# Two expert layers computed for sorted token-expert pairs in blocks of 128, in place of eight dense experts

## Chip, cores and metric

The kernel runs on one core of one Trainium2 chip. Its time is the device time of one execution, in microseconds (us). A core has TensorE (PE, matmuls; the load of their stationary operand is PEld), VectorE (DVE), ScalarE (ACT), GpSimd (POOL) and SyncE (SP, which here only issues transfers), each with a queue of its own that it works off strictly in order. They meet by semaphores.

## The reference, cut to what matters

The input is x, 4 sequences of 512 tokens of 128 numbers, in float32. Eight layers follow one another, each as x = x + layer(layernorm(x)): 0 a state space with 16 heads, 1 a feed forward, 2 a Mamba block, 3 experts with gelu, 4 linear attention with 16 heads, 5 a ternary feed forward, 6 a scan (called the last scan here), 7 experts with a silu gate. The two expert layers are what changes:

```
# layer 3: 8 experts, 128 -> 512 -> 128, the two most probable of each token count
probs = softmax(x @ Wr.T); topv, topi = top_k(probs, 2)
combine = sum(topv[..., None] * one_hot(topi, 8), axis=2)
for each expert e:  h = gelu(x @ w1[e] + b1[e]);  y = h @ w2[e] + b2[e]
                    out += combine[..., e, None] * y
# layer 7: the same with topv / sum(topv), and
g = x @ w_gate[e] + b_gate[e];  u = x @ w_up[e] + b_up[e]
y = (silu(g) * u) @ w_down[e] + b_down[e];  out += combine[..., e, None] * y
```

Written like this every expert is computed for every token, though only two of eight weights in `combine` differ from zero.

## The kernel before

**Tiles and streams.** P = 128, T = 512 tokens of a sequence, NC = 4 chunks of 128 tokens. x stays in SBUF (`x0` to `x3`). Two sequences are worked on at once, as stream 0 and stream 1; sequences 0 and 1 go through all eight layers (the first round), then 2 and 3 (the second round, with the same buffers). Each stream has four PSUM banks. In the tables of the trace buffer numbers are left out: `big`, `cv`, `mt`, `up`, `key`, `xT` stand for tiles that both streams have.

**What sets the order.** For every engine a layer is a generator that yields before each step. `walk(engine, programs)` runs the generators of both streams through each other by a table `RUNS[engine]`: the lengths of alternating runs of steps, stream 0, stream 1, stream 0 and so on. So each engine's queue is a fixed interleaving of two streams, written down ahead. Nothing overtakes at run time: a step that waits holds all that stands behind it on its engine, of the other stream too. The same helper `expert_loads()` gives the order in which SP brings expert weights into `expert_ring`, four slots for both streams.

**An expert layer before.** The layer norm and its transposes give `xT` (features on partitions, 512 tokens). `route` makes the logits (PE L1557), the softmax and the two largest (DVE L1172 to L1192), and spreads them as weights of eight experts, `cmb` (DVE L1196 and L1199). PE transposes `cmb` (L1562), ACT copies it (L748), and PE multiplies it with the experts' second biases (L1363, out of `rows8`). Then for each of the 8 experts:

- gelu layer: four matmuls 128x512 (L1606), four ACT activations 128x512 (L760), `down`: 16 matmuls 128x128 (L1363, by `by_token`), and on DVE `gated_sum`, four operations 128x128 that add the result times the token's weight to x (L1214).
- silu layer: eight matmuls 128x512 (L1626), four activations (L773), four DVE products 128x512 (L1237), then `down` and `gated_sum` as above.

A matmul in float32 is two instructions in the trace. SP loads 512 KB (gelu) or 768 KB (silu) for each expert.

**The other layers** that the text speaks of: a Mamba block is 16 steps a stream of DVE scans (L1137), a product (L1147) and POOL work (L563, L551), and ends in the output matmul (PE L1363 out of `weights` and `big`); attention works in eight groups of two heads (one PE L1643 each, among others), the ternary layer is mostly PE L1685, the state space has PE L1415, the last scan L1697 and others. POOL L517 computes the layer norms' 1/sqrt.

Of the kernel before, what the change touches and what calls it, by code (L numbers as in the profile page):

```python
# [35 lines left out]
NE = 8  # L36
DI = 1024
# [18 lines left out]
for _k, _w in WCOLS:  # L56
# [6 lines left out]
         ("mb1", 32), ("w1_s", 4), ("w2_s", 4), ("h1_s", 4), ("h2_s", 4), ("normw", 2),  # L63
         ("bg", 32), ("bu", 32), ("alpha", 1), ("beta", 1), ("a0", 1), ("w3_s", P)]
# [7 lines left out]
CCOLS = [("ident", P), ("tri", T), ("iota8", NE), ("pos", T), ("m_ref", REF + 64), ("mod128", T),  # L72
# [4 lines left out]
for _k, _w in CCOLS:  # L77
# [14 lines left out]
RING = 4  # L92

# [68 lines left out]
def expert_loads():  # L162

    met = [0] * NS
    order = []
    for s in turns("loads"):
        n = met[s] // NE
        order.append((n % 2, s + NS * (n // 2), met[s] % NE))
        met[s] += 1
    return order  # L170
# [1673 lines left out]
```

## Time and profile before

| | us |
|---|---|
| median of 3 runs | 1624.49 (1623.52 to 1625.1) |
| the profiled execution | 1621.69 |
| its span in the trace | 1619.8 |
| granted TensorE clock, mean | 0.911 of full speed |

The profile's first part gives each engine's busy time and instructions. Its second part cuts the span into 40 slices of 40.5 us, with a digit for the busy tenths of each engine, and PEclk for the clock that TensorE was granted. The chain that ended last is followed back from the last instruction; "issue" in it is time in which the engine waited for nothing that the profile shows. In the groups of instructions each row has the operation, its tiles and shapes, the count, then busy time, the mean of one in ns, and the idle time of the engine just before them with what ended most of it.

### The profile page before, as it was taken

What the parts mean: (1) busy time and instruction counts of PE and PEld (TensorE: products, weight loads), DVE (VectorE), ACT (ScalarE), POOL (GpSimd) and SP (SyncE); (2) the same over time, 40 slices, a digit from 0 to 9 for tenths busy, and PEclk for the clock granted to TensorE, in tenths of its full rate; (3) what the DMA queues carried; (4) which work ended last, traced back from release to release, by engine and by line L of the source; (5) the groups of instructions that cost most, each with busy time, mean ns of one, the idle gap of its engine ahead of it and who ended that gap; (6) DMA issues with size and microseconds to landing.
All of it is one profiled execution on the core that took longest, in us unless ns stands there. A gap on an engine that the chain in (4) does not pass through costs nothing.

```text
span 1619.8 us, 15913 instructions
## 1 busy us (share of the span) xinstructions
PE 1364.0 (84%) x5628; PEld 812.9 (50%) x5628; DVE 992.1 (61%) x2001; ACT 742.7 (46%) x1083; POOL 227.6 (14%) x192
## 2 busy tenths in 40 slices
PE   1986754569999979999689987998797799998998
PEld 0534511136766555655364554566333475555665
DVE  4676699978562464425647996457998427513533
ACT  1532474348434333244546873753586533234322
POOL 0100025634000000010001441000144000000000
PEclk9997866669999998999899997999898899997999
DMA  7000000001112000210001110110000021100211
GB/s 311 0 1 0 1 0 0 1 0 53 53 39 72 20 0 20 79 59 0 1 1 39 40 39 14 39 42 25 1 1 0 14 79 39 39 20 20 79 59 46
DMA packets 13446, 54.51 MB, mean 34 GB/s; under 512 B 1320, under 2 KB 3496, under 8 KB 12976
## 3 DMA queue, kind: packets, MB, share of 16 engines
q1 hardware_dynamic: 12784, 48.55, 9.1%
q10 hardware_dynamic: 576, 4.87, 0.7%
q8 instruction: 47, 0.77, 0.2%
q14 instruction: 39, 0.32, 0.1%
HBM read 52.37 MB, written 1.05 MB: 33 GB/s over the span
## 4 chain that ended last, share of the span: by engine, by line
PE 57%; DVE 11%; ACT 8%; issue 4%; POOL 1%; DVEq 0%; ACTq 0%; POOLq 0%
PE ps L1363 16%; PE ps L1626 12%; PE ps L1606 6%; PE ps L1685 5%; DVE up L1137 2%; PE ps L1415 2%; PE ps L1655 2%; PE ps L1674 2%; PE ps L1723 1%; PE ps L1643 1%; PE ps L1527 1%; PE ps L1354 1%; PE ps L1697 1%; ACT L739 1%; DVE big L1147 1%
## 5 line engine op out<-in xcount | busy, mean ns | idle before, releaser
L1363 PEld LDWEIGHTS ps<-expert_ring,big 128*128 128x128 f32 x2048 | 239.6, 193 | 32.4 <-issue 25.4
L1626 PE MATMUL ps<-xT,expert_ring 128*128 128x512 f32 x512 | 241.4, 611 | 12.6 <-ACT cv L773 9.9
L1363 PE MATMUL ps<-expert_ring,big 128*128 128x128 f32 x2048 | 241.0, 276 | 5.0 <-DVE x L1214 5.0
L517 POOL TENSOR_TENSOR rstd<-ve,nhalf 128x4 f32<-128x4 f32 x44 | 47.7, 1085 | 1010.7 <-DVE ve L931 843.6
L1137 DVE TENSOR_TENSOR_SCAN up<-cv,big 128x512 f32<-128x512 f32 x128 | 173.1, 1392 | 9.1 <-ACT cv L739 8.1
L1214 DVE SCALAR_TENSOR_TENSOR x<-ps,cmb,x 128x128 f32<-128x128 f32 x256 | 71.8, 342 | 171.0 <-PE ps L1363 170.2
L773 ACT ACTIVATE cv<-ps,params 128x512 f32<-128x512 f32 x128 | 86.8, 687 | 177.4 <-PE ps L1626 177.2
L1626 PEld LDWEIGHTS ps<-xT,expert_ring 128*128 128x128 f32 x512 | 94.4, 193 | 123.6 <-issue 95.1
L1237 DVE SCALAR_TENSOR_TENSOR big<-ps,params,cv 128x512 f32<-128x512 f32 x128 | 95.0, 746 | 84.6 <-PE ps L1626 82.1
L760 ACT ACTIVATE big<-ps,params 128x512 f32<-128x512 f32 x128 | 85.8, 687 | 95.6 <-PE ps L1606 95.0
L1606 PE MATMUL ps<-xT,expert_ring 128*128 128x512 f32 x256 | 126.6, 619 | 3.1 <-ACT big L760 2.8
L1544 PE MATMUL ps<-q,row_pick 96*128 96x512 bf16 x128 | 57.0, 459 | 72.8 <-DVE big L1147 51.8
L563 POOL TENSOR_TENSOR big<-big,mt 128x512 f32<-128x512 f32 x64 | 86.4, 1351 | 220.1 <-DVE up L1137 134.3
L1685 PE MATMUL ps<-big,weights 128*128 128x512 f32 x256 | 115.6, 593 | 0.0
L739 ACT ACTIVATE cv<-big,nega 128x512 f32<-128x512 f32 x128 | 88.2, 716 | 19.6 <-DVE up L1137 17.5
L1363 PE MATMUL ps<-weights,big 128*128 128x128 f32 x608 | 80.3, 290 | 12.9 <-DVE big L1160 8.7
L1363 PEld LDWEIGHTS ps<-weights,big 128*128 128x128 f32 x608 | 76.6, 204 | 25.7 <-DVE big L1160 10.3
L1527 PE MATMUL ps<-big,consts 128*128 128x512 f32 x128 | 83.3, 738 | 4.3 <-DVE big L1147 4.3
L551 POOL TENSOR_TENSOR mt<-mt,big 128x512 f32<-128x512 f32 x60 | 78.5, 1310 | 35.2 <-DVE big L1147 34.9
L1655 PE MATMUL ps<-qkv_parts,selectors_rounded 128*128 128x512 f32 x192 | 72.7, 490 | 9.6 <-DVE up L1273 7.0
L1544 PEld LDWEIGHTS ps<-q,row_pick 96*128 96x128 bf16 x128 | 13.8, 109 | 133.0 <-DVE big L1147 82.2
L1415 PE MATMUL ps<-big,mt 128*128 128x512 f32 x160 | 74.0, 619 | 2.7 <-ACT big L641 2.7
(232 smaller groups left out, 2010.6 us busy)
## 6 DMA issues: line engine op xcount, KB each, us to landing
expert_ring<-in_e_dram SPq DMA_DIRECT2D x32, 768.0 KB, 4.3
expert_ring<-in_e_dram SPq DMA_DIRECT2D x32, 512.0 KB, 3.6
weights<-in_w_dram ACTq DMA_DIRECT2D x1, 3072.0 KB, 13.3
weights<-in_w_dram SPq DMA_DIRECT2D x1, 1600.0 KB, 13.6
big<-in_sel_dram SPq DMA_DIRECT2D x1, 1024.0 KB, 7.6
x<-in_x_dram SPq DMA_DIRECT2D x4, 256.0 KB, 12.2
out_dram<-x SPq DMA_DIRECT2D x4, 256.0 KB, 5.7
big<-in_c_dram SPq DMA_DIRECT2D x1, 1008.0 KB, 10.2
```

The source lines that it names most:

```text
L563: pool.tensor_tensor(BIG2[s][:, 1, :], BIG1[s][:, 3, :], MT[s][:, 0:T], ALU.mult).then_inc(m_d1[s], 1)
L739: act.activation(CV[s][:, j, :], BIG1[s][:, j, :], ACT.Exp, scale=nega[:, j * NM + n:j * NM + n + 1]).then_inc(m_da[s], 1)
L773: act.activation(CV[s][:, k % 2, :], bank(s, (8 * e + 2 * k) % 3), ACT.Silu, bias=pr("bg", 4 * e + k)).then_inc(g.act[s], 1)
L1137: dve.tensor_tensor_scan(UP[s][:, j, PAD:PAD + T], CV[s][:, j, :], BIG2[s][:, j, :], 0.0, ALU.mult, ALU.add).then_inc(m_scan[s], 1)
L1237: dve.scalar_tensor_tensor(BIG1[s][:, 4 * (e % 2) + k, :], bank(s, (8 * e + 2 * k + 1) % 3), pr("bu", 4 * e + k), CV[s][:, k % 2, :], ALU. ...
L1363: last = pe.matmul(bank4(s, k)[:, c, :], lhs(b, c), rhs(b), start=(b == 0), stop=(b == blocks - 1))
L1415: last = pe.matmul(bank(s, c), MT[s][:, m:m + P], BIG2[s][:, k, :], start=(k == 0), stop=(k == c))
L1527: pe.matmul(bank(s, 0), ident, BIG2[s][:, 2, :], start=(n == 0), stop=(n == NM - 1))\
L1606: pe.matmul(bank(s, k % 3), ring[:, slot, k * P:(k + 1) * P], XT[s][:, PAD:PAD + T], start=True, stop=True).then_inc(g.up[s], 1)
L1626: pe.matmul(bank(s, b % 3), ring[:, slot, r * T + k * P:r * T + (k + 1) * P], XT[s][:, PAD:PAD + T], start=True, stop=True).then_inc(g.up[ ...
L1655: last = pe.matmul(bank(s, k), SELR[:, m * P:(m + 1) * P], PARTS[:, part, src, :], start=(part == 0), stop=(part == 1))
L1685: last = pe.matmul(bank(s, j), w(name, (4 * b + j) * P, P), BIG1[s][:, src + b, :], start=(b == 0), stop=(b == 3))
```

## The change

Both expert layers compute only the chosen token-expert pairs, 1024 for a sequence. NBLK = 15 blocks of 128 slots each hold pairs of one expert: 1024/128 = 8 full blocks and up to 7 more since each expert's last block may be partly filled. Which expert a block belongs to is known only at run time.

- `route` ends otherwise: DVE makes one-hots of the two choices (`oneh`, `chosen`); PE counts and ranks them with small bfloat16 matmuls (a triangle `trib`, ones `oneb`); some 13 small DVE operations turn that into the expert of each block (`whoi`) and each pair's slot (`posu`, 8 columns of 128). The transposes of `cmb`, its copy and the bias matmul go.
- POOL issues 8 indirect transfers (L653) that scatter the normalised tokens (`cv`) to rows of a DRAM buffer `slots0` or `slots1`, one a stream; SP reads them back in 4 transfers (L567), PE transposes 15 blocks (L1720), ACT copies them (L847).
- For each block SP loads the expert's number from SBUF into a register (L559), and issues the weights' transfer at that address (L561): 592 KB for gelu, 856 KB for silu, both biases included. PE: 4 (gelu) or 8 (silu) matmuls 128x128 (L1761), ACT 4 activations 128x128 (L876, L873), for silu 4 DVE products 128x128 (L1373), PE 4 matmuls 128x128 (L1734), DVE one addition of the bias into `YS` (L1337). 
- SP writes the results to a DRAM buffer in 4 transfers (L571), POOL gathers each token's two results with 8 indirect transfers (L660) into `up`, and DVE adds them to x by 8 operations 128x128 (L1346).
- SP clears both slot buffers once at the start, 983 KB each. The ring's slot frees when `result` has been computed (`y`) instead of with the down matmuls (`dn`).
- All tables in RUNS are new, for the other layers too; "loads" becomes "sp", an order of all that SP does.

```diff
+NBLK = 2 * T // P + NE - 1
+SP_MOE = ["w0", "w1", "x0", "x1", "x2", "x3", "w2", "w3", "w4", "w5", "w6", "w7", "y0", "w8", "w9", "w10", "w11",
+          "y1", "w12", "w13", "w14", "y2", "y3"]
 RUNS = {
...
-    "loads": [
-        8, 8, 8, 8, 8, 8, 8, 8],
+    "sp": [
+        1, 1, 21, 1, 1, 1, 1, 21, 19, 2, 4, 8, 1, 14, 23, 23, 19, 2, 4, 8, 1, 14],
 }
...
 SP:
-                    sp.wait_ge(moe[pm].dn[pi], moe[pm].dn.at(pi, pe_))
-                dst = ring[:, q % RING, :] if m else ring[:, q % RING, 0:1024]
-                sp.dma_start(dst, (e3_d if m else e1_d)[e]).then_inc(ring_in[q % RING], 16)
+                            if n == 0:
+                                sp.wait_ge(g.eb[s], g.eb.at(s, 0))
+                            if q >= RING:
+                                pm, pi, pb = loads[q - RING]
+                                sp.wait_ge(moe[pm].y[pi], moe[pm].y.at(pi, pb))
+                            e = sp.value_load(whoi[s][0:1, n:n + 1], min_val=0, max_val=NE - 1)
+                            src = (e3_d if m else e1_d)[bass.ds(e, 1)].rearrange("o p n -> p (o n)")
+                            sp.dma_start(ring[:, q % RING, 0:EW[m]], src).then_inc(ring_in[q % RING], 16)
...
+                        if label[0] == "x":
+                            if n == 0:
+                                sp.wait_ge(scattered[s % NS], 128 * (nth_moe(m, s) + 1))
...
 POOL:
+                    for j in range(2 * NC):
...
+                        pool.indirect_dma_start(xs_d[k], bass.IndirectOffsetOnAxis(ap=posu[s][:, j:j + 1], axis=0),
+                                                XH[s][:, j % NC, :], None).then_inc(scattered[k], 16)
+                    for j in range(2 * NC):
...
+                        pool.indirect_dma_start(YG[s][:, j // NC, (j % NC) * P:(j % NC + 1) * P], None, ys_d[k],
+                                                bass.IndirectOffsetOnAxis(ap=posu[s][:, j:j + 1], axis=0))\
...
 DVE:
-                for e in range(NE):
-                    if e:
-                        yield from gated_sum(0, s, e - 1)
-                yield from gated_sum(0, s, NE - 1)
+                for b in range(NBLK):
+                    yield from result(0, s, b)
+                yield from gated_sum(0, s)
...
 PE:
+                            if r == 0:
+                                pe.wait_ge(ring_in[q % RING], 16 * (q // RING + 1))
+                                if b % 4 == 0:
+                                    pe.wait_ge(g.gt[s], g.gt.at(s, b // 4))
+                                if m and b:
+                                    pe.wait_ge(g.act[s], g.act.at(s, b - 1))
+                            elif b:
+                                pe.wait_ge(g.h[s], g.h.at(s, b - 1))
+                            for k in range(4):
+                                last = pe.matmul(bank4(s, r if m else b % 2)[:, k, :],
+                                                 ring[:, q % RING, r * T + k * P:r * T + (k + 1) * P],
+                                                 XGT[s][:, b // 4, b % 4 * P:(b % 4 + 1) * P], start=True, stop=True)
```

What stands in a row on PE, first round, from the Mamba output of stream 0 (`weights,big2_0`) into its gelu experts, beside stream 1's Mamba steps (`row_pick`, `big2_1`). Before:

```order
L1363 MATMUL ps<-weights,big2_0 128x128 x8
L1544 MATMUL ps<-q128_1,row_pick 128x512
L1527 MATMUL ps<-big2_1,consts 128x512
L1544 MATMUL ps<-q128_1,row_pick 128x512
L1354 MATMUL ps<-consts,cv0 128x128 x4
L1557 MATMUL ps<-weights,xT0 128x8 x4
L1544 MATMUL ps<-q128_1,row_pick 128x512
L1527 MATMUL ps<-big2_1,consts 128x512
L1544 MATMUL ps<-q128_1,row_pick 128x512
L1562 MATMUL ps<-consts,cmb0 8x128 x4
L1363 MATMUL ps<-rows8,bT0 128x128 x4
L1606 MATMUL ps<-xT0,expert_ring 128x512 x2
```

After, where the slots of stream 0 are transposed and its first blocks start:

```order
L1681 MATMUL ps<-q128_1,row_pick 128x512 x2
L1664 MATMUL ps<-big2_1,consts 128x512
L1681 MATMUL ps<-q128_1,row_pick 128x512 x2
L1664 MATMUL ps<-big2_1,consts 128x512
L1720 MATMUL ps<-consts,big2_0 128x128 x8
L1761 MATMUL ps<-big1_0,expert_ring 128x128 x4
L1720 MATMUL ps<-consts,big2_0 128x128 x7
L1761 MATMUL ps<-big1_0,expert_ring 128x128 x4
L1664 MATMUL ps<-big2_1,consts 128x512
L1734 MATMUL ps<-expert_ring,big1_0 128x128 x4
L1761 MATMUL ps<-big1_0,expert_ring 128x128 x4
L1734 MATMUL ps<-expert_ring,big1_0 128x128 x4
```

The experts of stream 0 now begin late in stream 1's Mamba steps, behind a transfer to DRAM and back, and stand among its last steps.

What stands in a row on PE near the end of the program, the silu experts of stream 0 and then of stream 1. Before:

```order
L1363 MATMUL ps<-rows8,bT1 128x128 x4
L1626 MATMUL ps<-xT1,expert_ring 128x512
L1363 MATMUL ps<-expert_ring,big1_0 128x128 x16
L1626 MATMUL ps<-xT1,expert_ring 128x512 x15
L1363 MATMUL ps<-expert_ring,big1_1 128x128 x16
L1626 MATMUL ps<-xT1,expert_ring 128x512 x8
L1363 MATMUL ps<-expert_ring,big1_1 128x128 x16
```

After:

```order
L1761 MATMUL ps<-big1_0,expert_ring 128x128 x8
L1734 MATMUL ps<-expert_ring,big1_0 128x128 x8
L1720 MATMUL ps<-consts,big2_1 128x128 x8
L1761 MATMUL ps<-big1_1,expert_ring 128x128 x8
L1720 MATMUL ps<-consts,big2_1 128x128 x7
L1761 MATMUL ps<-big1_1,expert_ring 128x128 x8
L1734 MATMUL ps<-expert_ring,big1_1 128x128 x4
```

Before, stream 1's experts follow on stream 0's; after, all 15 blocks of stream 1 stand alone behind the last of stream 0, and the first waits for the slots to come back.

What stands in a row on POOL at the end of the program. Before:

```order
L517 TENSOR_TENSOR rstd0<-ve0,nhalf 128x4
L551 TENSOR_TENSOR mt1<-mt1,big2_1 128x512
L517 TENSOR_TENSOR rstd1<-ve1,nhalf 128x4
L517 TENSOR_TENSOR rstd0<-ve0,nhalf 128x4 x2
L517 TENSOR_TENSOR rstd1<-ve1,nhalf 128x4 x5
```

After:

```order
L589 TENSOR_TENSOR rstd0<-ve0,nhalf 128x4 x3
L589 TENSOR_TENSOR rstd1<-ve1,nhalf 128x4
L653 DMA slots0_dram<-cv0,key0 1920x128 x8
L589 TENSOR_TENSOR rstd1<-ve1,nhalf 128x4 x3
L653 DMA slots1_dram<-cv1,key1 1920x128 x8
L660 DMA up0<-results0_dram,key0 128x128 x8
L660 DMA up1<-results1_dram,key1 128x128 x8
```

Where only the layer norms' operations stood, 32 indirect transfers stand between and behind them, and a gather of one stream can stand behind a scatter of the other.

## Rows read from the trace of the kernel before

**Rows 1.** The page's first part, engines, and its second part's granted clock.

```profile
PE 1364.0 (84%) x5628; PEld 812.9 (50%) x5628; DVE 992.1 (61%) x2001; ACT 742.7 (46%) x1083; POOL 227.6 (14%) x192
...
PEclk9997866669999998999899997999898899997999
```

**Rows 2.** The page's costliest groups of instructions; columns as told above.

```profile
L1626 PE MATMUL ps<-xT,expert_ring 128*128 128x512 f32 x512 | 241.4, 611 | 12.6 <-ACT cv L773 9.9
L1363 PE MATMUL ps<-expert_ring,big 128*128 128x128 f32 x2048 | 241.0, 276 | 5.0 <-DVE x L1214 5.0
...
L1214 DVE SCALAR_TENSOR_TENSOR x<-ps,cmb,x 128x128 f32<-128x128 f32 x256 | 71.8, 342 | 171.0 <-PE ps L1363 170.2
...
L1237 DVE SCALAR_TENSOR_TENSOR big<-ps,params,cv 128x512 f32<-128x512 f32 x128 | 95.0, 746 | 84.6 <-PE ps L1626 82.1
...
L1606 PE MATMUL ps<-xT,expert_ring 128*128 128x512 f32 x256 | 126.6, 619 | 3.1 <-ACT big L760 2.8
```

**Rows 3.** The chain of waits: start, length, what; two stretches late in the program.

```profile
1411.08 27.47 PE ps L1685 x64
...
1600.41 6.87 PE ps L1626 x16
1607.29 3.58 PE ps L1363 x32
```

**Rows 4.** The page's DMA issues: count, KB each, us from issue to landing.

```profile
expert_ring<-in_e_dram SPq DMA_DIRECT2D x32, 768.0 KB, 4.3
expert_ring<-in_e_dram SPq DMA_DIRECT2D x32, 512.0 KB, 3.6
```

**Rows 5.** Timeline, Mamba output to the first expert: start, length, engine, operation.

```profile
328.41 3.78 PE L1363 MATMUL ps<-weights,big 128*128 128x128 f32 x16 [5.50 <-DVE big L1160]
...
339.45 1.87 PE L1557 MATMUL ps<-weights,xT 128*128 128x8 f32 x8 [0.69 <-ACT xT L625]
...
342.50 0.18 DVE L1178 RECIPROCAL sm<-sm 128x4 f32<-128x4 f32 x1
342.71 0.19 DVE L1179 TENSOR_TENSOR lg<-lg,sm 128x32 f32<-128x32 f32 x1
...
344.02 0.18 DVE L1192 CAST topf<-topi 128x32 f32<-128x32 uint32 x1
...
349.86 1.22 PE L1606 MATMUL ps<-xT,expert_ring 128*128 128x512 f32 x1
```

**Rows 6.** Timeline of POOL, one operation in two places.

```profile
211.07 1.27 POOL L563 TENSOR_TENSOR big<-big,mt 128x512 f32<-128x512 f32 x1 [4.70 <-DVE big L1124]
...
278.17 2.03 POOL L563 TENSOR_TENSOR big<-big,mt 128x512 f32<-128x512 f32 x1 [1.22 <-DVE up L1137]
```

**Rows 7.** All transfers that store the output: us to landing.

```profile
DMA to landing us min/median/max: 2.3/5.7/5.8
```

**Rows 8.** Timeline of PE: attention groups, the last scan, the state space's start and second product.

```profile
561.72 1.02 PE L1643 MATMUL ps<-up,selectors 128*128 128x512 f32 x2
562.58 3.60 PE L1697 MATMUL ps<-xT,weights 128*128 128x512 f32 x8
...
571.80 1.02 PE L1643 MATMUL ps<-up,selectors 128*128 128x512 f32 x2
...
598.56 2.03 PE L1363 MATMUL ps<-weights,big 128*128 128x128 f32 x16
...
710.92 0.60 PE L1354 MATMUL ps<-consts,cv 128*128 128x128 f32 x4
...
787.22 10.46 PE L1415 MATMUL ps<-big,mt 128*128 128x512 f32 x20 [0.69 <-ACT big L641]
```

**Rows 9.** Windows: length, busy (count) of PE, PEld, DVE, ACT, POOL, clock, DMA share, GB/s.

```profile
40.00:200.00 160.00, 129.45 (x518) 76.50 (x517) 103.82 (x204) 63.65 (x101) 14.79 (x16) 0.88 0.00 1
208.00:408.00 200.00, 127.60 (x393) 61.88 (x394) 183.12 (x233) 108.85 (x156) 88.93 (x64) 0.72 0.04 11
```

**Rows 10.** Timeline of DVE at the start, behind a register load and a branch.

```profile
32.67 0.87 DVE L936 BATCH_NORM_STATS2 stat<-x 128x6 f32<-128x128 f32 x4 [7.24 <-issue]
```

More of the change, by code:

```diff
@@ L162, in expert_loads, with network @@
 def expert_loads():
+    labels = [[None] + [(m, i, label) for i in range(k, NB, NS) for m in range(2)
+                        for label in SP_MOE + ["out"] * m] for k in range(NS)]
     met = [0] * NS
     order = []
[L166 to L169, printed above, removed]
+    for k in turns("sp"):
+        if met[k] < len(labels[k]):
+            label = labels[k][met[k]]
+            if label and label[2][0] == "w":
+                order.append((label[0], label[1], int(label[2][1:])))
+        met[k] += 1
     return order
-def network(nc, x_d, w_d, p_d, c_d, sel_d, a_d, e1_d, e3_d, r8_d, out_d, layers=NLAYERS):
+def network(nc, x_d, w_d, p_d, c_d, sel_d, a_d, e1_d, e3_d, r8_d, xs_d, ys_d, out_d, layers=NLAYERS):
     ctx = ExitStack()
@@ new lines, in route @@
+                step(dve.tensor_reduce(used, cnt4[s][:, :, :], AX.X, ALU.add))
+                step(dve.tensor_tensor_scan(ends, ones[:, 0:1].broadcast_to([P, NE]), used, 0.0, ALU.mult, ALU.add))
+                dve.tensor_tensor(past[s][:, :, :], ends[0:1].unsqueeze(1).broadcast_to([1, NBLK, NE]),
+                                  cn("blocks", 1)[:, 0:NBLK].unsqueeze(2).broadcast_to([1, NBLK, NE]), ALU.is_le)
+                step(dve.tensor_tensor(first, ends, used, ALU.subtract))
+                dve.tensor_reduce(whof[s][:, 0:NBLK], past[s][:, :, :], AX.X, ALU.add)
@@ new lines, in result, with gated_sum @@
+                dve.tensor_tensor(YS[s][:, group % 2, cols], bank4(s, 2 + b % 2)[:, 0, :], ring[:, slot, EW[m] - P:EW[m]],
+                                  ALU.add)\
+                    .then_inc(g.y[s], 1)
+            def gated_sum(m, s):
+                for r in range(2):
+                    yield
+                    dve.wait_ge(gathered[s % NS][r], 64 * (nth_moe(m, s) + 1))
+                    for c in range(NC):
+                        last = dve.scalar_tensor_tensor(X[s][:, c, :], YG[s][:, r, c * P:(c + 1) * P],
+                                                        top[s][:, c, r:r + 1], X[s][:, c, :], ALU.mult, ALU.add)
+                    if r == 0:
+                        step(last)
+                    else:
+                        last.then_inc(x_done[7 if m else 3][s], 1)
@@ L1612, in experts_silu @@
[L1612 to L1630 removed]
+                pe.wait_ge(g.mk[s], g.mk.at(s, 0))
@@ new lines, in route, with turn_slots @@
+                last.then_inc(g.rk[s], 1)
+            loads = expert_loads()
+            def turn_slots(g, s, k):
+                yield
+                pe.wait_ge(xg_in[s % NS][k], 16 * (nth_moe(moe.index(g), s) + 1))
+                if k >= 2:
+                    pe.wait_ge(g.gt[s], g.gt.at(s, k - 2))
+                elif k == 1:
+                    pe.wait_ge(g.pos[s], g.pos.at(s, 0))
+                for b in range(min(4, NBLK - 4 * k)):
+                    last = pe.transpose(bank4(s, 2 + k % 2)[:, b, :], XG[s][:, k, b * P:(b + 1) * P], ident)
+                last.then_inc(g.tr[s], 1)
@@ new lines, in down @@
+            def down(m, s, b):
+                g = moe[m]
+                wd = ring[:, loads.index((m, s, b)) % RING, 512 * (m + 1):512 * (m + 2)]
+                yield
+                hidden = g.h if m else g.act
+                pe.wait_ge(hidden[s], hidden.at(s, b))
+                if b >= 2:
+                    pe.wait_ge(g.y[s], g.y.at(s, b - 2))
+                else:
+                    pe.wait_ge(g.gt[s], g.gt.at(s, 2 + b))
+                for k in range(4):
+                    last = pe.matmul(bank4(s, 2 + b % 2)[:, 0, :], HID[s][:, b % 4, k * P:(k + 1) * P],
+                                     wd[:, k * P:(k + 1) * P], start=(k == 0), stop=(k == 3))
+                last.then_inc(g.dn[s], 1)
@@ L1750, in _ @@
                 first_block_general(pe, "pe", state_space(True))
-            walk("pe", [state_space(False), feed_forward, mamba, experts_gelu, attention, ternary, last_scan,
-                         experts_silu])
+            walk("pe", [state_space(False), feed_forward, mamba, experts(0, "r1"), attention, ternary, last_scan,
+                         experts(1, "r3")])
 def layout(i):
```

370 lines of the change are left out of this document (215 added, 155 removed), and 72 rows, old and new, of the table RUNS.

## The prediction, written before the changed kernel ran

> **What bounds the kernel now.** Read first the busy shares [rows 1]: TensorE 1364.0 of the span's 1619.8 us, no other engine near. Then the granted clock [rows 1]: where its digit is 6, PE is the less busy engine and DVE the busy one (in the window 208:408 DVE 183.12 of 200, PE 127.60, clock 0.72) [rows 9]; so the Mamba stretches are DVE's, nearly all the rest PE's. Then the costliest groups [rows 2]: the expert layers are 241.4 + 126.6 + 241.0 = 609 us of PE. The chain near its end [rows 3] shows them back to back: 6.87 up and 3.58 down for each silu expert, no gap. There a matmul less is time less.
>
> **What goes.** An old silu expert is 10.44 us of PE, a gelu expert 3.44 + 3.57 = 7.0 (half the up matmuls of rows 3). DVE loses 71.8 + 95.0 [rows 2].
>
> **What comes, on PE.** 16 matmuls 128x128 take 3.58 (x32 there, two records each) [rows 3], 0.223 each. A new gelu block has 8, 1.79 us; a silu block 12, 2.68; 30 + 30 blocks and 120 transposes of 0.15 or so: some 300 us with the group's mean of 0.235 for the 1200 (241.0/1024). PE busy falls from 1364 to about 1065. If PE alone set the time, the gain would be 300 us; I expect less than half of it, because each expert layer now holds a round trip that no engine computes in.
>
> **Routing.** From the start of the Mamba output to `topf` 15.6 us (328.41 to 344.02) and to the first expert 21.4 [rows 5]. New behind `topf`: about 14 dependent small DVE operations at 0.21 from one to the next (342.50 to 342.71), a small PE step with two hops, ~5 in all. Positions stand at +20.6; bounds 18 to 24, with up to three of the other stream's DVE operations of about a microsecond between them.
>
> **The round trip.** No row shows an indirect transfer. The nearest rows of POOL's queue are its own operations: L563, 1.27 alone and 2.03 beside a busy DVE [rows 6]. A zero-cost issue would be the lower end, and nothing excludes it; I take 1.3, the undisturbed row of the same engine for a 128-row operation, with bounds 0.4 to 2.03. Eight are 10.4, and landing 2.3 (the shortest of the stores) [rows 7]: 12.7 for a scatter and for a gather. Slots come back in 3, transposes and copy 1.7. Positions to first block 17.4, so Mamba output to first block 38 (21.4 before). Behind the last block: last down and its addition 1.2, result write 2.7 (0.4 more than the 2.3), gather 12.7, eight additions at 0.342 (L1214) [rows 2] 2.7: **19 us**, against four such, 1.4, before. POOL's queue behind a scatter holds the other stream's 1/sqrt of the layer norm (the order on POOL), up to 10 us; most of those are far apart.
>
> **SP.** Each block adds a register load and an issue, in one queue for both streams. The nearest row is DVE's 7.24 at the start, a register load with a branch [rows 10]; the lower end is an ordinary issue, ~0.35. I take 1.0. The Trainium skill, "DMA: Bandwidth & Descriptors" (Latency and other measured facts), gives a `tensor_load` a floor of about 600 ns; no run here shows it, and by it the loads would hide. Weights: 592 and 856 KB against 512 in 3.6 and 768 in 4.3 [rows 4], where 256 KB more cost 0.7: so 3.8 and 4.5 to land, and 1.6 and 2.3 of the transfer engines each, below a block's pace. 87 MB in all (41 before) is no limit.
>
> **Pace of blocks.** In-order downs and the ring of four tie block q to block q-4: SP 1.35, landing 3.8 or 4.5, up 0.9 or 1.8, four activations of 128 columns 1.4 (taken as DVE's of that width), down 0.9, addition 0.3: 8.7, and for silu 11.6 with DVE's four products. Over four blocks that is 2.2 and 2.9; with hops **2.4 for gelu, 3.0 for silu**; bounds 1.8 and 2.7 (PE) to 3 and 3.6. Eight old experts were 56 and 84; fifteen blocks are 36 and 45. Alone, a gelu layer goes 21.4 + 56 + 1.4 = 79 to 38 + 36 + 19 = 93, longer; a silu layer 107 to 102. What is won is PE time for the other stream during the round trips, so the gain hangs on what stands beside them. Therefore a walk through the new orders.
>
> **The walk.** Legs from rows: two of attention's eight groups in 10.1 (561.72 to 571.80) [rows 8], eight 40, some 10 around them, 7 for the layer norm (332.2, the output matmul's end, to 339.45) [rows 5]: 57; ternary 32 matmuls 27.47 [rows 3], 40 with the tail and layer norm 45 to 53; last scan 36 (562.58 to 598.56) [rows 8], 42 to 51 with what surrounds it; state space to its second product 76 (710.92 to 787.22) [rows 8], 32 more to its output; DVE per stream for state space and feed forward 103.82/2 = 52, for a Mamba block ~88 [rows 9].
> First round: the Mamba output of stream 0 comes at 345 (328 before: the new order on PE lets stream 1 go ahead by some 3.5 steps, at 88/16 less its share of other work about 4.7 each). Slots 388 (38, and 5 behind stream 1's steps in the order on PE); blocks to 424; x 443; attention 500; ternary 553; last scan 598; ternary of stream 1 to 638; its scan 689; its slots 727. Stream 0's silu blocks run meanwhile and give x at 735; its second-round state space starts at 742, second product 818. Stream 1's last downs stand behind that product: 829; state space out 850.
> Second round: Mamba of stream 0 beside state space and feed forward of stream 1, DVE 88 + 52, with its waits 145: 995. Slots 1033, blocks 1069, x 1088, attention 1145. Stream 1's Mamba output 1135, slots 1173, blocks 1209, rest of ternary 0 to 1233, last scan 1282, ternary 1 to 1330, its scan 1381, slots 1419, fifteen silu blocks alone to 1464, gather and sum 1483, store 2.4 [rows 7] 1485; and the 1.9 by which the profiled time (1621.69) exceeds its span: **1487**, against 1621.69, whose distance to the median of 1624.49 is 0.2%.
> As a cross-check: 1065 of PE in 1487 is 72%, so the gaps grow from 256 to 422 us. The granted clock would then fall: windows with PE near 64% show 0.72 [rows 9]. A fall of mean clock from 0.91 to 0.87 costs 5% of about 600 us where PE binds, 30 us, inside my range.
>
> **The rivals.** (a) POOL is held by DVE. If the indirect transfers behave as L563 beside DVE, 2.03 each [rows 6], the walk holds nine groups of eight: 72 x 0.75 = 54, **1541**. For it: round trips stand beside Mamba steps, where DVE is at 92%. Against: the last ones stand where DVE idles. The Trainium skill, "DMA: Bandwidth & Descriptors" (SWDGE vs HWDGE vs iDMA), says GpSimd writes such descriptors into SBUF and that DVE locks it out in its two-port modes; no row of before has such a transfer to show it.
> (b) Blocks at PE's pace and cheap transfers: 0.6 less for each of the 30 gelu blocks on the path of the second round and 0.3 for some 30 silu blocks, 27, and 0.7 for each of 72 transfers, 50: **1410**. For it: nothing in the trace forbids an issue of 0.6.
> (c) Slower: the register load on SP, price p for each block. SP then gives one slot every p + 0.35, for both streams; a block lasts 2.4 to 3.0, so up to p = 2.2 nothing changes, and above it about 90 block times on the path grow. The gain of 138 is used up at 138/90 = 1.5 more, p about 4. At the 7.2 of rows 10 the 60 blocks of the two lone stretches and the shared ones cost 90 x 4.7 = 420: **1905**. Against it: those 7.24 have a branch and a start in them, and no row shows a load by itself that dear.
> (d) The exchange doesn't pay: orders that hold a stream's work behind the other's slots eat the gain, round trips growing by 17 us in all eight layers (8 x 17 = 136): **1622**, no change.
>
> **How the numbers follow.** Forecast 0.60 (its own range 1445 to 1530), (a) 0.14, (b) 0.13, (c) 0.08, (d) 0.05. The range 1395 to 1580 takes in the forecast, (a), (b) and their bounds and leaves out (c), (d) and the tails: about 8 in 10. Faster by over 0.2% (about what a measurement of this kernel can tell from no change): 0.60 + 0.14 + 0.13 + half of (d) = 0.89; within 0.2%: 0.01; slower: 0.10.
>
> **What would show it.** PE busy 1040 to 1090, DVE about as before (it loses 167, gains some 130 in blocks and sums). POOL's timeline: eight transfers in 9 to 12 us (a: above 16). Between the last `topf` and the first L1761: 20 to 25. Block pace in the last silu layer: 3.0; if it is 4 or more and the ring's landing ends the waits, (c). The last 19 us of the span: no PE. In the second round the Mamba stretch of DVE should stand nearly as before; if it shrinks or grows by over 20 us, my legs are wrong, not the prices. Wrong I would also be if a scatter to DRAM took far longer to land than the 2.3 of a plain store: 5 us more would be 9 x 5 = 45.

## The result, and the profile after

| | before | after |
|---|---|---|
| median, us | 1625.10 (1622.38 to 1629.41, 15 runs) | 1634.78 (1627.51 to 1639.36, 15 runs) |
| ratio | | 1.0046, 95% interval 1.003 to 1.0062 |
| span of the profiled execution | 1619.8 | 1633.4 |
| granted TensorE clock, mean | 0.911 | 0.826 |

The changed kernel is half a per cent slower, by more than its interval. The forecast was 1487. All times here and below are of undisturbed executions, two to eight for most versions; of `ring8_small` there is only one (its other ran at a granted clock of 0.594 and took 2057).

The page's first part and the granted clock, after (they answer to [rows 1]):

```profile
PE 1157.1 (71%) x5300; PEld 760.8 (47%) x5300; DVE 955.1 (58%) x2083; ACT 646.5 (40%) x1274; POOL 369.1 (23%) x321
...
PEclk9998757556998989886897777767877998897788
```

TensorE lost 207 us of busy time, and more than that came back as idle time: 476 us without a matmul against 256. The clock is below full through most of the program. Its costliest groups and the issues of weights (to [rows 2] and [rows 4]):

```profile
L1761 PE MATMUL ps<-big,expert_ring 128*128 128x128 f32 x1440 | 212.0, 300 | 97.8 <-DMA expert_ring<-in_e_dram 80.7
...
L1734 PE MATMUL ps<-expert_ring,big 128*128 128x128 f32 x960 | 130.5, 280 | 8.5 <-ACT big L876 7.4
...
L660 POOL DMA_INDIRECT up<-results_dram,key x64 | 62.4, 975 | 219.2 <-DMA results_dram<-mt 199.5
...
L653 POOL DMA_INDIRECT slots_dram<-cv,key x64 | 66.1, 1033 | 103.3 <-DVE key L1324 86.8
...
expert_ring<-in_e_dram SPq DMA_DIRECT2D x60, 836.0 KB, 4.7
expert_ring<-in_e_dram SPq DMA_DIRECT2D x60, 578.0 KB, 4.6
```

The first row's last part is the news: 97.8 us in which PE stood idle ahead of a block's up matmuls, 80.7 of them for expert weights to land. Before, experts' matmuls waited 12.6 + 3.1 + 5.0 us in all [rows 2], and PE's list of waits has none for a load of weights.

Where the time went along the program, read from the start of each layer norm's transposes on PE (L1354 before, L1491 after; an apostrophe marks the second round; the forecast's column is its walk, with the 7 to 10 us of a layer norm added where it named the end of a layer). The last two columns are versions told of below:

| start of | before | forecast | after | sp_order | ring5 |
|---|---|---|---|---|---|
| attention, stream 0 | 437 | 450 | 464 | 465 | 458 |
| state space', stream 0 | 711 | 742 | 794 | 765 | 749 |
| feed forward', stream 0 | 842 | 857 | 898 | 870 | 851 |
| gelu experts', stream 0 | 991 | 1005 | 1086 | 1056 | 1037 |
| attention', stream 0 | 1105 | 1095 | 1194 | 1163 | 1145 |
| silu experts', stream 1 | 1505 | 1388 | 1506 | 1472 | 1449 |
| end | 1620 | 1485 | 1633 | 1570 | 1541 |

The forecast's lead is lost in three places: 38 us ahead of the second round (stream 0's and stream 1's silu experts), 40 between feed forward' and gelu experts', 30 behind the last layer norm; the rest in pieces of 14 to 19, less 11 that the state space' wins back.

### The profile page after: what moved, and what is told of

Read it like the earlier page. It is cut to its first block and busy times, and to the rows that moved or that the text cites. A ratio compares the mean times of both kernels' runs of the same rounds, so it can differ in the third digit from the quotient of the medians.

```text
span 1633.4 us, 16356 instructions
## 1 busy us (share of the span) xinstructions
PE 1157.1 (71%) x5300; PEld 760.8 (47%) x5300; DVE 955.1 (58%) x2083; ACT 646.5 (40%) x1274; POOL 369.1 (23%) x321
## 5 line engine op out<-in xcount | busy, mean ns | idle before, releaser
L1761 PE MATMUL ps<-big,expert_ring 128*128 128x128 f32 x1440 | 212.0, 300 | 97.8 <-DMA expert_ring<-in_e_dram 80.7
L1761 PEld LDWEIGHTS ps<-big,expert_ring 128*128 128x128 f32 x1440 | 193.3, 211 | 115.4 <-DMA expert_ring<-in_e_dram 89.8
L1244 DVE TENSOR_TENSOR_SCAN up<-cv,big 128x512 f32<-128x512 f32 x128 | 181.4, 1456 | 15.3 <-POOL big L635 12.2
L1373 DVE SCALAR_TENSOR_TENSOR big<-ps,expert_ring,key 128x128 f32<-128x128 f32 x240 | 67.6, 344 | 140.4 <-PE ps L1761 125.3
L635 POOL TENSOR_TENSOR big<-big,mt 128x512 f32<-128x512 f32 x64 | 87.9, 1379 | 226.2 <-ACT mt L828 114.7
L1734 PE MATMUL ps<-expert_ring,big 128*128 128x128 f32 x960 | 130.5, 280 | 8.5 <-ACT big L876 7.4
L1734 PEld LDWEIGHTS ps<-expert_ring,big 128*128 128x128 f32 x960 | 120.5, 196 | 17.3 <-ACT big L876 12.8
L873 ACT ACTIVATE key<-ps,expert_ring 128x128 f32<-128x128 f32 x240 | 68.4, 368 | 147.5 <-PE ps L1761 147.1
L660 POOL DMA_INDIRECT up<-results_dram,key x64 | 62.4, 975 | 219.2 <-DMA results_dram<-mt 199.5
L828 ACT ACTIVATE mt<-ps 128x512 f32<-128x512 f32 x64 | 38.4, 600 | 144.9 <-PE ps L1681 123.2
L1337 DVE TENSOR_TENSOR mt<-ps,expert_ring 128x128 f32<-128x128 f32 x120 | 34.3, 287 | 98.1 <-PE ps L1734 97.8
L653 POOL DMA_INDIRECT slots_dram<-cv,key x64 | 66.1, 1033 | 103.3 <-DVE key L1324 86.8
L876 ACT ACTIVATE big<-ps,expert_ring 128x128 f32<-128x128 f32 x240 | 67.9, 374 | 53.2 <-PE ps L1761 53.0
```

The source lines that it names most:

```text
L635: pool.tensor_tensor(BIG2[s][:, 1, :], BIG1[s][:, 3, :], MT[s][:, 0:T], ALU.mult).then_inc(m_d1[s], 1)
L873: last = act.activation(SG[s][:, b % 2, cols], bank(s, 0)[:, cols], ACT.Silu, bias=bias[:, k:k + 1])
L876: last = act.activation(HID[s][:, b % 4, cols], bank(s, b % 2)[:, cols], ACT.Gelu, bias=bias[:, k:k + 1])
L1244: dve.tensor_tensor_scan(UP[s][:, j, PAD:PAD + T], CV[s][:, j, :], BIG2[s][:, j, :], 0.0, ALU.mult, ALU.add).then_inc(m_scan[s], 1)
L1734: last = pe.matmul(bank4(s, 2 + b % 2)[:, 0, :], HID[s][:, b % 4, k * P:(k + 1) * P], wd[:, k * P:(k + 1) * P], start=(k == 0), stop=(k == 3))
L1761: last = pe.matmul(bank4(s, r if m else b % 2)[:, k, :], ring[:, q % RING, r * T + k * P:r * T + (k + 1) * P], XGT[s][:, b // 4, b % 4 * P ...
```

## Experiments

Times are medians; "after" is 1634.8. A difference of a few us between two versions with two executions each is within the spread. Kernels that leave work out say so in their expectation.

### Whose slots: the order on SP

The end of the program in after. First SP's issues of weights from 1506 on (start, length, queue, operation), then DVE's results of blocks 11 and 12 of stream 0, each of which frees a slot, and PE's up matmuls with their waits:

```profile
1508.58 0.33 SPq L561 DMA_DIRECT2D expert_ring<-in_e_dram  x1
...
1516.95 0.33 SPq L561 DMA_DIRECT2D expert_ring<-in_e_dram  x1
...
1518.12 2.74 SPq L561 DMA_DIRECT2D expert_ring<-in_e_dram  x2
...
1534.37 0.34 SPq L561 DMA_DIRECT2D expert_ring<-in_e_dram  x1
```

```profile
1519.48 0.28 DVE L1337 TENSOR_TENSOR mt<-ps,expert_ring 128x128 f32<-128x128 f32 x1
...
1528.17 3.79 PE L1761 MATMUL ps<-big,expert_ring 128*128 128x128 f32 x16 [8.88 <-DMA expert_ring<-in_e_dram]
...
1533.03 0.28 DVE L1337 TENSOR_TENSOR mt<-ps,expert_ring 128x128 f32<-128x128 f32 x1
...
1539.38 3.41 PE L1761 MATMUL ps<-big,expert_ring 128*128 128x128 f32 x16 [6.44 <-DMA expert_ring<-in_e_dram]
...
1562.93 3.58 PE L1761 MATMUL ps<-big,expert_ring 128*128 128x128 f32 x16 [5.79 <-DMA expert_ring<-in_e_dram]
...
1573.25 3.54 PE L1761 MATMUL ps<-big,expert_ring 128*128 128x128 f32 x16 [5.85 <-DMA expert_ring<-in_e_dram]
```

Read them together. At 1508.58 SP loads block 12 of stream 0; at 1516.95 and 1518.12 come blocks 0 and 1 of **stream 1**, whose slots in DRAM are not even written yet. PE starts on the first of them at 1550.67, 34 us later, and their slots are loaded anew only at 1558.51 and 1568.66: two of the four slots are held all that time. So stream 0's block 13 may load only when block 11 is done (1519.48; PE runs block 13 at 1528), and block 14 when block 12 is done (1533.03; PE runs block 14 at 1539). PE does block b-1's down matmuls only behind block b's up matmuls, so each such load is waited for in full: about 11 us a block in place of 3. Then the same again for stream 1: its loads 2 and 3 fall into the slots of its own blocks 0 and 1 (PE at 1562.9 and 1573.2).

```diff
     "sp": [
-        1, 1, 21, 1, 1, 1, 1, 21, 19, 2, 4, 8, 1, 14, 23, 23, 19, 2, 4, 8, 1, 14],
+        1, 1, 21, 1, 1, 1, 1, 21, 21, 2, 2, 8, 1, 14, 23, 23, 21, 2, 2, 8, 1, 14],
```

> The changed kernel with one thing moved: on SP the weights of stream 0's last two silu blocks (13 and 14) are issued ahead of stream 1's first two, in both rounds. Theory 'ring in a row' (the changed kernel loses in its silu layers because SP holds those two loads behind stream 1's routing, and because stream 1's loads 2 and 3 then land in the slots of its own blocks 0 and 1): the trace of after shows PE idle for 8.9 and 6.4 us ahead of the one, 5.8 and 5.8 ahead of the other, 27 in the second round and about as much in the first, so 1635 becomes about 1590 (1580 to 1605). Rival 'round trips' (what is lost is lost in transfers to and from DRAM and beside DVE): less than 8 us of change, since no transfer is shortened.

Measured: **1576.5**, ratio to before 0.9704 (0.9675 to 0.9734); 58 us less than after, and 3.5 below the low end of what was expected. PE's wait for weights, after and then sp_order (waits of PE: total, times, longest):

```profile
PE ps L1761 <- DMA expert_ring<-in_e_dram: 80.7, 42, 8.9
```

```profile
PE ps L1761 <- DMA expert_ring<-in_e_dram: 32.1, 36, 3.1
```

Two numbers of a table, in each round, and the change is worth 3% where it cost half a per cent. For these 58 us the rival "round trips" is out: no transfer was shortened.

### Queue or slots: four against eight

```diff
-EW = (1024 + 4 + P, 1536 + 8 + P)
+EW = (512 + 8 + P, 512 + 8 + P)
...
-                            src = (e3_d if m else e1_d)[bass.ds(e, 1)].rearrange("o p n -> p (o n)")
+                            src = (e3_d if m else e1_d)[bass.ds(e, 1), :, 0:EW[m]].rearrange("o p n -> p (o n)")
```

> The changed kernel with smaller weights transfers: one matrix of 512 columns for each block (325 KB in place of 578 or 836), from which up, gate and down are all computed; ring of four as it is, same work on all engines. A control for the next run. Theory 'ring in a row': the waits are for the issue and the order, not for the bytes: landings shrink from 4.7 to about 3 us, so 10 to 25 less than after (1634.8), the 8.9 and 6.4 us ahead of the last blocks of stream 0 still there. Rival 'bandwidth' (111 MB of weights): 50 or more less.

Measured: 1598.9, 36 less than after: more than the 10 to 25 expected, less than the rival's 50. (The weights of after are 87 MB; 111 MB is all that SP's queue moves.) Loads land sooner (median 3.1 us against 4.7 and 4.6), and since each wait in the starved stretches is one landing, that counts: PE's wait for weights went from 80.7 to 43.1.

```diff
-RING = 4
+RING = 8
```

> As ring4_small, with a ring of eight slots (which fit at that size); SP's order is unchanged. Theory 'ring in a row' has two parts: SP's queue (loads 13 and 14 of stream 0 behind the wait for stream 1's routing), which eight slots don't mend, and the slot order (loads 2 and 3 of stream 1 behind its own blocks 0 and 1), which they do. So about half of what the changed SP order gave: 15 to 35 less than ring4_small, with the wait ahead of stream 0's last blocks still in the trace. If all 58 us of the SP order's gain come back here, it was the slots alone; if under 8, the queue alone.

Measured: 1543.2, in one execution, 56 less than ring4_small: nearly all that the SP order gave. Of the theory's two parts the slots are by far the larger. With eight slots and SP's order unchanged, this is left of the wait for weights (total, times, longest; ahead of it PE's three longest waits; then the first of its two places):

```profile
PE ps L1681 <- DVE big L1254: 106.4, 28, 12.9
PE ps L1491 <- DVE cv L1049: 62.0, 13, 20.9
PE ps L1681 <- DVE big L1236: 17.7, 12, 2.8
...
PE ps L1761 <- DMA expert_ring<-in_e_dram: 6.4, 2, 3.5
```

```profile
716.67 3.41 PE L1761 MATMUL ps<-big,expert_ring 128*128 128x128 f32 x16 [3.48 <-DMA expert_ring<-in_e_dram]
```

That place is stream 0's block 13 of the silu layer, whose load SP issues right behind stream 1's first two, when stream 1's routing is done (DVE L1319 at 708.81). So the queue part exists, at 3.5 and 2.9 us for the two rounds. In after it doesn't show at the end of the program: there SP's wait for stream 1's routing (DVE L1319 at 1514.91) ended a microsecond before the slot that it needed came free (1515.87).

> ring8_small (small weights transfers, eight slots) with the changed order on SP of sp_order as well. ring4_small to ring8_small gave 56 us, sp_order 58. If both take away the same thing (loads of one stream that hold or lack a slot), they don't add up: 1533 to 1548, at most 10 less than ring8_small (1543). If SP's queue is a cause of its own, they add up in part: below 1525.

Measured: 1530.2, 13 less than ring8_small, between the two expectations (at most 10 less; below 1525). Most of what the two remedies take away is the same, since 56 and 58 don't add up. Both of PE's remaining waits for weights are gone, 6.4 us; where the other 7 come from was not isolated, and they rest on one execution of ring8_small.

### What the new operations cost by themselves

```diff
+                        if j:
+                            continue
                         pool.indirect_dma_start(xs_d[k], bass.IndirectOffsetOnAxis(ap=posu[s][:, j:j + 1], axis=0),
...
+                        if j % NC:
+                            continue
                         pool.indirect_dma_start(YG[s][:, j // NC, (j % NC) * P:(j % NC + 1) * P], None, ys_d[k],
```

> The changed kernel with 1 indirect transfer in place of 8 for each scatter and 2 in place of 8 for each gather (the others are left out, so most slots hold old rows; all waits stay in their place). On POOL that takes 7 x 1.26 = 8.8 and 6 x 1.25 = 7.5 us out of each of 8 layer passes, 130 in all. Theory 'round trips' : most of it is on the path, 100 to 130 less, about 1515. Theory 'ring in a row' with 'beside DVE': half of them or fewer have nothing late behind them, 40 to 80 less, about 1575.

The counts that SP and DVE wait for are lowered to match. Measured: 1602.4, 32 less, a quarter of the 130 us that POOL no longer spends. It stands below what either theory said. By the layer norms' starts, 14 us of it lie in stream 0's gelu layer of the second round, 8 in the last silu layer, the others give 4 at most: elsewhere the other stream's work covers the round trip.

> sp_order with 1 indirect transfer in place of 8 for a scatter and 2 in place of 8 for a gather (the rest left out). In the changed kernel itself that gave 32 us of the 130 that went from POOL. If transfers had been hidden behind the waits for slots, they come out now: 50 to 80 less than sp_order (1576.5), the two silu layers of a round giving 8 us at each side. If not, the same 25 to 40.

Measured: 1547.7, 29 less than sp_order, where 32 came from the same cut in after. Transfers and the order on SP don't hide one another.

```diff
-                            e = sp.value_load(whoi[s][0:1, n:n + 1], min_val=0, max_val=NE - 1)
-                            src = (e3_d if m else e1_d)[bass.ds(e, 1)].rearrange("o p n -> p (o n)")
+                            src = (e3_d if m else e1_d)[n % NE]
```

> The changed kernel with expert n mod 8 for block n, fixed in the program, in place of the number that SP loads into a register (the computation is another). SP's register load, its address and its check take 0.27 + 0.15 + 0.02 us and about 0.5 with issue for each block in the trace of after. Theory 'register loads cost' (rival c of the prediction): tens of us less, 40 or more. All other theories: at most 60 x 0.5 x the fifth of blocks that wait on SP, 3 to 10 us less.

Measured: 1620.2, 15 less; somewhat over the 3 to 10 expected, and far from rival (c). SP's row for the register loads in after (min/median/max):

```profile
L559 SPq TENSOR_LOAD <-key x120: 262/268/1087, 372.7 to 1604.8; - x120
```

0.27 us each, where the prediction took 1.0 for the whole and allowed up to 7.2.

### What TensorE's work is worth

```diff
 by_token, for the experts' down matmuls only:
+                        if half and b % 2:
+                            continue
...
-                        pe.matmul(bank(s, k % 3), ring[:, slot, k * P:(k + 1) * P], XT[s][:, PAD:PAD + T],
+                        pe.matmul(bank(s, k % 3)[:, 0:T // 2], ring[:, slot, k * P:(k + 1) * P], XT[s][:, PAD:PAD + T // 2],
```

> The kernel before, with half of TensorE's expert work left out: up matmuls over 256 columns in place of 512, and every second of the down matmuls; order, loads, ACT and DVE work are as they were. It takes 609/2 = 305 us of PE out, what the change takes out, without round trip, ring or new order. Theory 'PE work was the time' (the reading of my forecast's first part): 250 to 300 less, 1330 to 1370. Theory 'beside DVE' (a good part of the expert work stood beside other engines' work that is as long): 120 to 200 less, 1425 to 1500.

Measured: **1469.0**, 155 less. The expectation counted 305 us of TensorE work; the profile shows that PE's busy time fell by 228 (1364.0 to 1136.2): the up matmuls of half the columns took 223 us and not 184, and at a mean clock of 0.881 in place of 0.911 the others took longer. So in the old order, with nothing added, 155 of 228 us of busy time came back, and half of what the count had promised; PE's idle time grew by 75.

```diff
-                            for k in range(4):
+                            for k in (0, 1, 2, 3, 0, 1, 2, 3):
```

> The changed kernel with each block's up matmuls issued twice over (the same result twice): 720 matmuls 128x128 more, 720 x 0.235 = 170 us of TensorE at the mean of the rows of before. Theory 'TensorE still sets the time': 140 to 180 more. Theory 'waits set it': a part of it disappears in idle time of PE, as in before_half_pe, where 305 us less work gave 155: 60 to 110 more. Under 40 more would say that TensorE's expert work is nowhere on the path.

Measured: 1742.6, 108 more for 170 of work as counted, at the upper edge of "waits set it"; PE's busy time grew by 141. So TensorE's expert work counts in either kernel at 0.5 to 0.6 of its time as counted beforehand, 0.7 to 0.8 of the busy time as measured; it is not the bound by itself.

### DVE under two streams

In the second round the new order lays stream 0's Mamba block beside stream 1's state space. Windows (length, busy and count of PE, PEld, DVE, ACT, POOL, clock, DMA share, GB/s): of before, from Mamba' to gelu experts' of stream 0; of after, from the state space' of stream 1 (its transposes start at 889.91) to gelu experts' of stream 0; of after, from feed forward' to gelu experts' of stream 0:

```profile
858.00:991.00 133.00, 115.38 (x464) 65.37 (x462) 116.86 (x175) 89.36 (x116) 45.31 (x38) 0.94 0.12 40
```

```profile
890.00:1086.00 196.00, 132.24 (x398) 65.56 (x398) 167.84 (x272) 97.86 (x141) 52.93 (x44) 0.75 0.00 0
```

```profile
898.00:1086.00 188.00, 126.41 (x389) 63.55 (x388) 162.12 (x258) 96.07 (x138) 48.05 (x39) 0.76 0.00 0
```

Before, Mamba' stood beside silu experts: PE 87% busy at clock 0.94, DVE 88%. After, DVE has both streams' work, 168 us in 196, while PE is busy for 132 at clock 0.75. Measured alike, from the Mamba block's own transposes (858.29 before, 921.24 after) to gelu experts', it takes 133 us before and 165 after.

```diff
-                        dve.tensor_tensor_scan(UP[s][:, j, PAD:PAD + T], CV[s][:, j, :], BIG2[s][:, j, :], 0.0,
+                        dve.tensor_tensor_scan(UP[s][:, j, PAD:PAD + T // 2], CV[s][:, j, 0:T // 2],
+                                               BIG2[s][:, j, 0:T // 2], 0.0,
```

> The changed kernel with Mamba's 128 scans on DVE over the first 256 of 512 columns (the rest is left out). The trace of after has them at 1.456 us each, so about 0.65 x 128 = 83 us of DVE work go, 42 for a round. Theory 'DVE under two streams' (the changed order lays stream 0's Mamba block of the second round beside stream 1's state space, both full of DVE work: DVE busy 167.8 of the 196 us from 890 to 1086): nearly all of it is on the path, 70 to 95 less. Rival 'TensorE still sets the time' (with its lower clock, 0.826): 20 to 50 less.

> The kernel before with the same cut of Mamba's scans. Theory 'DVE under two streams': only the first round's Mamba stretch, where DVE is at 92%, gives its share (42 us and less), the second, which stands beside silu experts, next to nothing: 35 to 55 less, clearly less than the changed kernel with the same cut. Rival: both kernels lose the same.

Measured: after 1589.3 (45 less), before 1595.6 (29 less). Both lie below the theory's ranges, and 45 is in the rival's ("TensorE still sets the time", 20 to 50). The changed kernel does gain more by the cut, but the stretch itself became only 8 us shorter for the 15 us of DVE time that went from it.

```diff
-                step(dve.scalar_tensor_tensor(v[:, j, :], u[:, j, 2:2 + T], pr(*wcol(2)), v[:, j, :], ALU.mult, ALU.add))
-                step(dve.scalar_tensor_tensor(v[:, j, :], u[:, j, 1:1 + T], pr(*wcol(1)), v[:, j, :], ALU.mult, ALU.add))
```

> The changed kernel with two of the four taps of each convolution on DVE left out (L1065 and L1066; 40 convolutions, 1.72 us each, 69 us of DVE). In the stretch from 890 to 1086 stand 12 of them, 20 us. Theory 'DVE under two streams': that stretch becomes 15 to 20 us shorter, the program 35 to 55. Rival 'fixed order' (each stream's chain through all engines sets it, DVE is merely busy): the stretch loses under 8 us, the program under 25.

> The kernel before with the same two taps left out. Its state spaces of the second round stand beside TensorE-heavy layers. Theory 'DVE under two streams': 15 to 35 us less, clearly less than the changed kernel. Rival 'fixed order': both kernels lose the same.

Measured: after 1610.8 (24 less), before 1612.5 (12 less, below its range). The program's gain is that of the rival, the stretch's that of the theory: it became 17 us shorter, as this window of after_half_conv shows, with DVE still at 84%:

```profile
885.00:1065.00 180.00, 122.50 (x400) 61.72 (x401) 150.63 (x250) 98.19 (x141) 52.97 (x44) 0.80 0.00 1
```

So in that stretch DVE's work is on the path, for convolutions nearly in full, for scans by half; of the 28 convolutions elsewhere 7 us came back. Why scans count for less was not settled.

### Towards a better kernel

```diff
                 for b in range(NBLK):
+                    if b:
+                        yield from result(1, s, b - 1)
...
                     last.then_inc(g.h[s], 1)
-                    if b:
-                        yield from result(1, s, b - 1)
```

> sp_order with one more thing: in the silu layers DVE adds the bias to block b-1's result, which frees its slot, ahead of block b's product instead of behind it. In the trace the result of TensorE is there 0.9 us after the up matmuls, while the product must wait for ACT's 1.14; so the slot is free 1.1 to 1.4 us earlier. Where a load is what ends the wait (in most of the 60 silu blocks, four blocks a cycle) that is 0.3 a block: 10 to 18 us less than sp_order (1576.5). If slots no longer hold anything up, under 4.

Measured: **1608.3**, 32 more than sp_order: a clear miss. DVE now waits for block b-1's down matmuls, and block b's product and the other stream's work are queued behind that wait. DVE's wait for L1734, sp_order and then result_first (total, times, longest):

```profile
DVE mt L1337 <- PE ps L1734: 100.4, 56, 10.4
```

```profile
DVE mt L1337 <- PE ps L1734: 193.9, 93, 10.2
```

And PE waits in turn for the product; in sp_order that wait (L1761 for DVE L1373) is 3.1 us in all:

```profile
PE ps L1761 <- DVE big L1375: 31.0, 29, 3.6
```

A step that frees a slot earlier is worth nothing if its own operand comes later than that of the step it overtakes.

```diff
-RING = 4
+RING = 5
...
-    nc = _bacc.Bacc("TRN2", target_bir_lowering=False, num_devices=1, dynamic_dma_scratch_size=8192)
+    nc = _bacc.Bacc("TRN2", target_bir_lowering=False, num_devices=1, dynamic_dma_scratch_size=2048)
```

> result_first with a ring of five full-size slots. The room comes from the scratch for POOL's descriptors, 2048 bytes in place of 8192. ring4_small to ring8_small gave 56 us with the old order on SP, 13 from there came from the order; at full size, with the order mended, I expect 15 to 30 less than result_first. If the small scratch makes the indirect transfers wait for one another, they show as more than 1.26 us from one to the next, and it gets slower.

Measured: 1585.8, 22.5 less than result_first, within the expectation.

> sp_order with five full-size slots in the ring (room from POOL's descriptor scratch, 2048 bytes in place of 8192), DVE's order as in the changed kernel. If the fifth slot's 23 us (1608.3 to 1585.8) are independent of DVE's order: 1545 to 1562. If they only paid back the waits that the reversed order made: within 8 us of sp_order (1576.5).

Measured: **1547.1** (1542.7 to 1552.0), ratio to before 0.9528 (0.951 to 0.9546), 29 less than sp_order, where 22.5 came with result_first's order: what the fifth slot gives doesn't hang on DVE's reversed order. PE's wait for weights is 6.2 us in all, 32.1 in sp_order. It computes all of the reference and is the fastest full kernel here: 4.7% faster than before, 5.4% faster than the changed kernel. The smaller scratch doesn't show in POOL's own time for a scatter (median 0.958 in both). The landing of a scatter is later in ring5 than in after (2.2/3.0/6.3), but not in result_ring5, which has the same small scratch (ring5, then result_ring5):

```profile
DMA to landing us min/median/max: 2.2/4.2/6.6
```

```profile
DMA to landing us min/median/max: 2.2/3.0/6.5
```

So the scratch isn't shown to be the cause. With the small weights of ring4_small and ring8_small the median is 2.3 and 2.4.

## Why the prediction was wrong, point by point

**What was right.** TensorE's matmuls fell as counted (their busy time less so, as told under the clock); positions took 24 us from the Mamba output (349.5 to 373.4; 20.6 forecast, 18 to 24 the bounds). The indirect transfers cost POOL what was taken: 0.96 us and 0.30 between two, 1.26 against 1.3; they land a little later, in 3.0 and 2.5 against 2.3. Rival (a) had a true mechanism at a small price: 7 of the 128 transfers took 1.48 to 1.92 us, each beside a DVE scan (L1244), but all 128 together took 128.5 us, about 7 more than at their medians, where (a) asked for 54. The last 19 us are 16.8 (1614.05 to 1630.81). The register load is 0.27; rival (c) had its price wrong by far. Yet the sign that the prediction gave for (c) did come: in the last silu layer PE started a block every 4.3 us (1550.67 to 1610.54), with landings ending the waits. fixed_expert and sp_order tell the two apart. The "30 + 30 blocks" are 60 + 60; the sum made from them is right.

**The step that failed first: "Pace of blocks".** It tied block q to block q-4 and took four slots as the block's own. With the slots well ordered that is right: in sp_order's last layer PE starts a block every 2.9 us (1509.28 to 1546.66, 13 blocks; 3.0 forecast). But the ring serves both streams, and a load issued ahead for one is a slot less for the other. I had read SP's order and counted its queue, not its slots. That is 58 of the 148 us by sp_order. A fifth slot gave 29 more, so in the better order four slots still held the two streams up.

**The walk's leg "Mamba beside state space, DVE 88 + 52, with its waits 145".** It measured 188, from the end of stream 0's state space output to its Mamba output in the second round of after:

```profile
884.20 3.84 PE L1500 MATMUL ps<-weights,big 128*128 128x128 f32 x32 [0.87 <-ACT big L783]
...
1076.47 1.95 PE L1500 MATMUL ps<-weights,big 128*128 128x128 f32 x16
```

DVE is busy for 162 of the 188 us of the window 898:1086, where 88 + 52 made 140: the leg left out that stream 0's own feed forward and the start of stream 1's Mamba block (its transposes at 1069.29) stand in it too. And 26 us of waits come on top, where 145 left 5. The prediction's own sign for wrong legs, a Mamba stretch grown by over 20 us, came (133 to 165). Neither the order on SP nor the fifth slot mends this leg (186 and 185 in the table's columns, 188 in after).

**"Positions to first block 17.4", beside Mamba.** POOL runs its Mamba steps between the transfers: the first scatter goes from 373.88 to 390.00, 16.1 in place of 10.4, by three such steps (3.9 us) and by four transfers that took 1.20 to 1.92. It is the only one: the other fifteen groups of eight took 9.7 to 11.1. Mamba output to first block was 47 (349.53 to 396.66), not 38. With the gelu layer of the second round (108 against 90) this is some 27 us. By few_transfers, the time that comes back when most transfers go is 32 for all eight layers.

**The clock.** The prediction let it fall to 0.87 and put that at 30 us, inside its range but not in its sum; it fell to 0.826. Busy time of PE is 92 us over the sum, 60 of it here: the 1200 matmuls of the blocks took 342.5 us, 282 at the mean of [rows 2]. In the stretch of waits 16 up matmul records took 3.79 us behind 8.88 idle (1528.17), in the packed stretch 1.95. These are the two levels of the clock, 1.2 and 2.4 GHz, as these windows of after show:

```profile
1528.00:1532.00 4.00, 3.83 (x18) 3.83 (x19) 0.01 (x1) 1.14 (x4) 0.00 (x0) 0.50 0.00 0
...
1577.00:1612.00 35.00, 30.15 (x261) 29.25 (x260) 14.38 (x55) 11.76 (x42) 0.00 (x0) 1.00 0.74 260
```

What it cost in time was not isolated.

**The balance.** before_half_pe says what the saved TensorE work is worth where it stood: 155, which would be 1470. The changed kernel lies 165 above that. Slots account for 88 (after to ring5), the number of transfers for about 30, register loads for 15; sp_order_few shows that the order on SP and the transfers add up (58 + 29 = 87 from after). About 32 are left for landings and the DVE stretch. The parts were measured one at a time and need not add up exactly; so the sum is a check, not a proof. Rival (d), "the exchange doesn't pay", came nearest in time (1622), with a chance of 0.05 and in part by luck: it rightly blamed the orders, but had all eight round trips longer, where the largest part was the order of loads into the ring.

## What to carry to other kernels

When two streams share a ring, count for every load how many blocks of its own stream lie between it and the load whose slot it takes; a prefetch whose data can't be used yet costs the other stream a slot. A busy share of 84% does not price an engine: halve its work in the old kernel first, which here would have said 155 us for the 305 that the count of matmuls promised, before any cost of the new scheme. And a layer that loses its TensorE work stops being cover for DVE-heavy work beside it, so the pairing has to be looked at anew.

## What was not expected of the hardware

An indirect transfer of 128 rows takes POOL 0.954 to 1.924 us as a scatter, median 0.958 (0.940 to 1.522 as a gather), with 0.30 from one to the next, and lands in 2.2 to 6.3; that is no dearer than POOL's own operation on 128x4 elements (1.12 on the mean in after). An SP register load from SBUF takes 0.27 us, below the floor of about 600 ns that the Trainium skill, "DMA: Bandwidth & Descriptors" (Latency and other measured facts), gives for a `tensor_load`; the measurement decides. Three of the 40 DVE operations of line L1065, with two inputs from SBUF, took 1.64 us in place of 0.75 (750/752/1637), at 966.31, 974.66 and 983.03 in after. These three, and none of the other 37, started while POOL ran L635; this was seen, not tested.
